# Weight loads of an attention block: the host lays Wk, Wv and Wo out so that each partition's row is one contiguous run

## The reference

```python
x = x + attn(layernorm(x), Wq, Wk, Wv, Wo)     # 32 query heads, 8 K/V heads of 128,
                                               # RoPE, causal window of 512, softmax, @ Wo
x = x + ffn(layernorm(x), qw_gate, qw_up, qw_down, s_*, z_*)
# ffn: W = (q - z) * s in groups of 128 (int4 values held in int32), 4096 -> 11008 -> 4096,
#      h = silu(x @ Wg.T) * (x @ Wu.T);  h @ Wd.T
```

## Time and profile before

| | us |
|---|---|
| runs shown | 10011.02, 10631.76, 10657.72 (median 10631.76) |
| the profiled execution | 10011.02 |
| its span, slowest core | 10009.4 |
| its span, fastest core | 9961.9 |
| TensorE busy | 5931.9 (59%) |
| VectorE busy | 2157.3 (22%) |
| ScalarE busy | 2258.1 (23%) |
| GpSimd busy | 154.6 (2%) |

### The profile page before, as it was taken

How to read it: one execution, slowest core, us unless ns; L and a number is a source line. 1 busy time by engine, 2 the same in 40 slices (tenths; PEclk the granted TensorE clock), 3 DMA queues, 4 the chain that set the end, 5 groups by cost and what they waited for, 6 DMA issues and landing times.

```text
span 10009.4 us, 81526 instructions; the slowest of 8 cores (9961.9 to 10009.4 us)
## 1 busy us (share of the span) xinstructions
PE 5931.9 (59%) x29632; PEld 2960.8 (30%) x29632; DVE 2157.3 (22%) x6972; ACT 2258.1 (23%) x4443; POOL 154.6 (2%) x188
## 2 busy tenths in 40 slices
PE   0000000233244567776667749999988699999886
PEld 0000000222212243321136624444433244444333
DVE  4555555444412212221100040000000000000000
ACT  3444444667613002234410030000000000000000
POOL 0000000000000000000000000000000000000000
PEclk9999999555566788876678859999999899999998
DMA  9999999999934233310034317777644388886443
GB/s 293 330 330 329 327 328 294 272 268 277 261 64 88 30 57 101 97 49 0 0 59 76 68 32 149 151 150 151 143 140 139 117 150 153 150 151 135 138 141 115
DMA packets 2161354, 1578.03 MB, mean 158 GB/s; under 512 B 1503040, under 2 KB 1966912, under 8 KB 2104384
## 3 DMA queue, kind: packets, MB, share of 16 engines
q1 hardware_dynamic: 1948832, 1201.60, 47.6%
q10 hardware_dynamic: 37152, 270.55, 7.0%
q0 software_dynamic: 174976, 100.68, 6.7%
HBM read 983.41 MB, written 295.70 MB: 128 GB/s over the span
## 4 chain that ended last, share of the span: by engine, by line
PE 51%; DMA 29%; DVE 7%; ACT 7%; issue 4%; SPq 2%; POOL 0%; ACTq 0%; DVEq 0%; POOLq 0%
PE pd L1104 12%; DMA scr_g<-wb_g 11%; PE pgg L1031 11%; PE puu L1039 10%; DMA qsl_d<-qd_in 7%; PE pq L711 5%; PE po L885 5%; DVE wb_g L247 3%; ACT wb_d L385 3%; DMA wgu_sl<-scr_u 2%; DMA x1t_sl<-scr_x1t 2%; PE pvv L582 2%; DMA wo_sl<-wo_t 2%; ACT probs L807 2%; PE ps_pv L773 1%
## 5 line engine op out<-in xcount | busy, mean ns | idle before, releaser
L324 PE MATMUL ptd<-ident,wb_d 128*128 128x128 bf16 x2752 | 303.3, 308 | 2420.2 <-ACT wb_d L385 2420.2
L1104 PE MATMUL pd<-hT,wd_sl 128*128 128x512 bf16 x5504 | 1208.0, 383 | 265.0 <-DVE out_st L1120 243.0
L1031 PE MATMUL pgg<-x2nT,wgu_sl 128*128 128x512 bf16 x5504 | 1224.4, 381 | 101.8 <-DMA wgu_sl<-scr_u 94.6
L1039 PE MATMUL puu<-x2nT,wgu_sl 128*128 128x512 bf16 x5504 | 1216.0, 379 | 0.0
L324 PEld LDWEIGHTS ptd<-ident,wb_d 128*128 128x128 bf16 x2752 | 284.2, 144 | 2439.0 <-issue 2439.0
L276 ACT ACTIVATE wb_u<-qsl_u,nzs_u,s_u 128x128 bf16<-128x128 int32 x1892 | 740.9, 481 | 894.3 <-DMA qsl_u<-qu_in 894.2
L247 DVE TENSOR_SCALAR wb_g<-qsl_g,s_g,nzs_g 128x128 bf16<-128x128 int32 x2752 | 712.6, 343 | 712.5 <-DMA scr_g<-wb_g 711.5
L1104 PEld LDWEIGHTS pd<-hT,wd_sl 128*128 128x128 bf16 x5504 | 542.3, 99 | 930.8 <-issue 293.9
L1031 PEld LDWEIGHTS pgg<-x2nT,wgu_sl 128*128 128x128 bf16 x5504 | 537.2, 98 | 767.6 <-issue 135.9
L1039 PEld LDWEIGHTS puu<-x2nT,wgu_sl 128*128 128x128 bf16 x5504 | 538.4, 98 | 649.5
L1051 ACT ACTIVATE sil_st<-pgg,c_zero 128x512 f32<-128x512 f32 x172 | 118.6, 689 | 2265.1 <-PE pgg L1031 2265.1
(11 more groups left out here) (97 smaller groups left out, 2958.3 us busy)
## 6 DMA issues: line engine op xcount, KB each, us to landing
qsl_g<-qg_in SPq DMA_DIRECT2D x86, 2048.0 KB, 35.4
qsl_u<-qu_in SPq DMA_DIRECT2D x86, 2048.0 KB, 42.5
qsl_d<-qd_in SPq DMA_DIRECT2D x86, 2048.0 KB, 16.6
wd_sl<-scr_d SPq DMA_DIRECT2D x80, 2048.0 KB, 9.3
scr_u<-wb_u ACTq DMA_DIRECT2D x86, 1024.0 KB, 17.9
scr_g<-wb_g ACTq DMA_DIRECT2D x86, 1024.0 KB, 27.1
scr_d<-sst ACTq DMA_DIRECT2D x86, 1024.0 KB, 11.4
wqf<-wq_t SPq DMA_DIRECT2D x256, 256.0 KB, 2.8
```

The lines of the kernel that those rows point to most:

```text
L324: last = tensor.transpose(ptd[it % 2][:, hs * 128:(hs + 1) * 128], wb_d[it % 2][:, hs * 128:(hs + 1) * 128], ident[:])
L1031: last = tensor.matmul(pgg[it % 2][:], wgu_sl[2 * (it % 2)][:, ht * 128:(ht + 1) * 128], x2nT[:, ht * TOK + tc * 512:ht * TOK + (tc + 1) * ...
L1039: last = tensor.matmul(puu[it % 2][:], wgu_sl[2 * (it % 2) + 1][:, ht * 128:(ht + 1) * 128], x2nT[:, ht * TOK + tc * 512:ht * TOK + (tc + ...
L1104: last = tensor.matmul(pd[:, oi * 512:(oi + 1) * 512], wd_sl[(og * NGRP + grp) % 2][:, gi * 1024 + oi * 128: gi * 1024 + (oi + 1) * 128], ...
```

## The change

The host lays the three weights out in the order in which SBUF holds them: for each load a [128, 4096] or [128, 8192] f32 block in which a partition's row is contiguous. The source of one load is now 128 runs, of 16 KB for wk_sl and 32 KB for wkv_sl and wo_sl, and the destination of each partition was contiguous already (8 KB or 16 KB in bf16). The number of loads, their bytes, their issuing engine, their waits and all compute instructions stay.

```diff
-    wk_t = dram_in("wk_t", [NKV, H, 128], F32)
-    wv_t = dram_in("wv_t", [4, H, 256], F32)
-    wo_t = dram_in("wo_t", [8, H, 512], F32)
+    wk_t = dram_in("wk_t", [NKV, 128, NHT * 128], F32)
+    wv_t = dram_in("wv_t", [4, 128, NHT * 256], F32)
+    wo_t = dram_in("wo_t", [8, 2, 128, NHT * 256], F32)
@@ p3a_gp, and the same in p3b_gp
-            P.inc(gpsimd.dma_start(
-                wk_sl.ap().rearrange("p (t q) -> p t q", q=128),
-                wk_t[kv].rearrange("(t p) q -> p t q", p=128)), "lKV", 16)
+            P.inc(gpsimd.dma_start(wk_sl[:], wk_t[kv]), "lKV", 16)
@@ emit_v, f_gp
-                P.inc(gpsimd.dma_start(
-                    wkv_sl.ap().rearrange("p (t q) -> p t q", q=256),
-                    wv_t[vc].rearrange("(t p) q -> p t q", p=128)), "lKV", 16)
+                P.inc(gpsimd.dma_start(wkv_sl[:], wv_t[vc]), "lKV", 16)
@@ p5b_gp
-                P.inc(gpsimd.dma_start(
-                    wo_sl[h % 3].ap().rearrange("p (t q) -> p t q", q=256),
-                    wo_t[oc].rearrange("(t p) q -> p t q", p=128)[:, :, half * 256:(half + 1) * 256]),
-                    "lo%d" % (h % 3), 16)
+                P.inc(gpsimd.dma_start(wo_sl[h % 3][:], wo_t[oc, half]),
+                      "lo%d" % (h % 3), 16)
@@ _host_inputs
-    wk_t = np.ascontiguousarray(wk.reshape(H, NKV, 128).transpose(1, 0, 2))
-    wv_t = np.ascontiguousarray(wv.reshape(H, 4, 256).transpose(1, 0, 2))
-    wo_t = np.ascontiguousarray(wo.reshape(H, 8, 512).transpose(1, 0, 2))
+    wk_t = np.ascontiguousarray(
+        wk.reshape(32, 128, 8, 128).transpose(2, 1, 0, 3)).reshape(8, 128, 32 * 128)
+    wv_t = np.ascontiguousarray(
+        wv.reshape(32, 128, 4, 256).transpose(2, 1, 0, 3)).reshape(4, 128, 32 * 256)
+    wo_t = np.ascontiguousarray(
+        wo.reshape(32, 128, 8, 2, 256).transpose(2, 3, 1, 0, 4)).reshape(8, 2, 128, 32 * 256)
```

## The result

The changed kernel takes 9919.86 us in the median of 12 runs (9894.75 to 10737.94), the kernel before 10161.25 in the median of its 12 (9985.83 to 10686.04). Compared among the other executions the ratio is 0.9898, with a 95% interval of 0.9879 to 0.9918. That is 1.0% faster, 102 us of 10011 (0.0102 x 10011), where the forecast was 79 to 81. The profiled execution went from 10011.02 to 9901.92 us.

A forecast was written before the change was run, and what follows sets the result against it. TensorE's open waits for the three weights, 526 of 10011 us, were taken as all the change can reach. The terms 21 + 18 + 35 + 8 - 3 = 79 us off gave 9932, stated as 9930 us, range 9862 to 10000.

The forecast's parts named there:

- The frame: TensorE's open waits for the three weights, 526 of 10011 us, are all that the change can reach.
- (a): Generation: GpSimd's DMA instruction for the three weights' loads gets 1.14 us shorter, and the data start moves with it.
- (b): Data: with long rows, generation included, wk_sl lands 1.5 us earlier (14 waits, 21 us), wkv_sl 2.3 (8 waits, 18 us).
- Rival 1: A load's start doesn't move with GpSimd's instruction, so 34 of the 79 us are not gained: 9966 us; chance 0.14.
- (c): Output projection: wo_sl's longer packets gain against x0c, 5 us for each of seven chunks (35) and 8 at the first wait.
- at most 27: Output projection: x0c lands later, at most about 27 us after its issue, with both wo_sl loads ahead of it.
- So it costs nothing: Output projection: x0c's later landing is free, since TensorE can do two tiles first, until 28.5 us against 27.
- (d): Start of p3a: the first wk_sl's long packets delay the first x0st tile, a loss of 0 to 5 us, 3 taken.
- Rivals 3 and 4: Cast rows cut back into small packets, 10011 us, chance 0.05; wide-pitch rows read at half rate, 10239 us, chance 0.05.

The follow-up runs named there:

- e3: Changed kernel with 32 to 1 runs a partition, by head, in wk_sl's loads (some wkv_sl too); halo landing 9.75 us with 32 runs, 7.98 with one.
- e5: Changed kernel without x0c's loads for chunks 1 to 7: seven wo_sl waits 94.4 us against 100.9; the kernel before, likewise cut: 116.3 against 147.2.
- e7: Changed kernel with x0c's source in rows of 16 KB too; the projection's seven chunks take 638.1 us in place of 610.1.
- e2: Kernel before with only wo_t laid out as in the change; stretch from first x0st issue to feed-forward part 3238.6 us against 3281.5.
- e4: Changed kernel with six memsets (1.6 us) on GpSimd ahead of each of 40 loads; K stages 171.7 to 187.9 and 229.5 to 246.0 us.
- e8: Changed kernel with two buffers each for the K and V weights; stretch to the feed-forward part 2870.6 us, 311.8 under the changed kernel's.

## Why the prediction came out as it did

- **The frame held.** Nearly all of the gain lies in the 526 us of open waits and in what hangs on them; the time is inside the stated range (9862 to 10000) and within 2% of the kernel before. The figure of 9930 stands 10 us over the median of all runs and about 21 over what the ratio gives (0.9898 x 10011 = 9909). It was a sum against the lowest of the three executions that were shown; beside their median of 10631.76 it reads as a forecast of 6.6%, which no term of it was: the sum claimed 0.8%, and 1.0% was measured. The figure's level was that of one execution; only the 79 us behind it were a forecast of what the change does.
- **(a) and (b) held.** wk_sl lands after 8.2 us (8.3 forecast), wkv_sl after 12.7 (13.1). A wait for wk_sl fell by 1.6 us (1.5 forecast), one for wkv_sl by 3.0 (2.3 forecast), so that term was 6 us too small. Rival 1, that the start of a load would not move with GpSimd's instruction, is wrong here: the first bytes come 1.2 us after the issue in place of 2.4, and e3 shows the wait following the instruction through 1.68, 1.14 and 0.88 us. The Trainium skill ("DMA: Bandwidth & Descriptors", section on the anatomy of a GpSimd DMA) calls descriptor generation small; here GpSimd's instruction is 1.1 of the 1.6 to 1.8 us that 4096 runs cost a wk_sl load, so the trace doesn't bear the page out.
- **(c) came out right in sum, 44.7 us against 43, partly by luck.** The queue with the longer packets wins (e5 to e7). I put wo_sl's gain from that at half; it won outright on four of the eight cores (waits of 13.8 to 14.6 us) and by the last chunk on all, and 42.1 us came for the seven waits instead of 35. The first wait gave 2.6 us where I had 8, and the two errors nearly cancel; the 43.5 us from which I took the 8 were core 3's, and the cores had 37.1 to 45.0. x0c's landing is 30.4 us, 3 over the "at most 27", and on core 7 that did reach TensorE, with 6.1 us in all. "So it costs nothing" was too sure: the margin was 1.5 us.
- **(d) held**: 2.7 us against 3, and e2 shows it gone when the first wk_sl has its short packets back. The later start of the load in e4 gave back 1.5 of it; what makes up the rest no run shows.
- **The step that failed** is the last sentence of the change part by part: "the 32 matmuls behind a wait take 9.8 us now, and I see no reason why 12 us of idleness ahead of them should leave them otherwise than 14 do". They take 8.4 to 8.7 us in most heads of the halo; core 6 of the changed kernel, two of them:

```profile
2856.37 8.44 PE L539 MATMUL pk<-x1nT_h,wk_sl 128*128 128x512 bf16 x32 [12.36 <-DMA wk_sl<-wk_t]
2876.95 8.38 PE L539 MATMUL pk<-x1nT_h,wk_sl 128*128 128x512 bf16 x32 [12.15 <-DMA wk_sl<-wk_t]
```

The granted clock of the K stages rose from 0.66 to 0.74 and from 0.73 to 0.78, and TensorE's busy time fell by 4.6 and 4.3 us in the median of the cores (by 7.8 and 4.5 between the two slowest cores). The two stages gained 37.6 us where 25.6 were forecast; of the 12, about 3 are waits that fell a little further than 1.5 and 2.3 us a load (the seven for wk_sl by 11.2 and 11.3 where 10.5 stood), and the other 9 are the clock. e4 turns that back with a delay alone. I had priced a wait at its own length and left out the matmuls behind it, a term that I put at nothing.
- **Rivals 3 and 4** didn't happen: the packets are one for each partition, and e3 finds no price for the pitch.

## What to carry to other kernels

When a load stands in the open between two groups of matmuls, cut it into instruction, start, data and landing before pricing a new layout: here more than half of what the layout gave a wk_sl load was GpSimd's instruction, which is longer the more runs there are, and 8 runs of 2 KB a partition had most of the gain. Look at what else is in flight: lengthening one queue's packets takes bandwidth from the other queue, which was a gain for wo_sl, a loss for x0st and x0c, and went into reverse as soon as x0c's packets were lengthened too. And an open wait is best removed, not shortened: on top of the layout, which brought 58 us for these loads, a second buffer brought about 300 more. Second buffers with the old layout were not tried.

## What the runs showed of the hardware

- wk_sl waits of 12.0 us leave TensorE at 0.74 of its full clock over the halo K stage (changed kernel, core 6), waits of 13.7 us at 0.67 (e4, core 6); 32 matmuls of 512 columns behind such a wait take mostly 8.4 to 8.7 us in the first and 8.4 to 10.0 in the second. In the own K stage with no wait for a load it is 0.97, and in five heads of the halo K stage of e8 (core 3), with waits of under 2 us or none ahead of them, 32 of them take 7.07 us.
- A casting load that GpSimd issues moves one packet a partition of 16 or 32 KB read when the source row is contiguous; its data take 6.4 to 6.5 us for 2 MB read (e3), against 7.0 to 7.2 in packets of 512 B.
- GpSimd's DMA instruction grows with the runs: 0.53 us for 128, 0.70 for 256, 0.75 for 512, 0.88 for 1024, 1.14 for 2048, 1.68 for 4096.
- Of two queues that share the 16 engines, the one with 2 KB packets landed its 2 MB after 10.8 us against 1 KB packets and after 30.4 against 32 KB packets.
